# The beginning of a three-part attention and expert kernel: constants moved into the first block, loads reordered and awaited by use

## The chip, the cores and the metric

One core of one Trainium2 chip runs the whole program. The metric is device time in microseconds (us) of one execution. Before the change three runs took 859.69, 860.32 and 865.04 us, so the median is 860.32 us. The engines are named as in the profile: PE is TensorE (matmul), PEld its weight loads, DVE is VectorE, ACT is ScalarE, POOL is GpSimd, SP is SyncE, which here only issues DMAs. SPq, ACTq and so on are the instruction sequencers of these engines.

## What is computed

The input x has 8 batches of 256 rows of 512 features, and there is a context of the same shape. Four residual layers follow each other:

```
x = x + L0_xattn(layernorm(x), ctx)     # latent cross attention, one 128-wide latent
x = x + L0_ffn(layernorm(x))            # gated feed-forward, fp8 operands
x = x + L1_xattn(layernorm(x), ctx, ctx)# 8 heads
x = x + L1_ffn(layernorm(x))            # 8 experts, top 2
```

The change touches only the first layer, and of it only the beginning. For one batch it is

```
theta = theta_w . input2 + theta_b              # input2 = ctx
phi   = phi_w . input1 + phi_b                  # input1 = layernorm(x)
p     = softmax(theta^T . phi)
g     = g_w . input1 + g_b
t     = p . g
h     = relu((t - mean) * rsqrt(var + eps) * ln_gamma + ln_beta)
out   = out_w . h + out_b + ctx
```

## The kernel before, in words

The program is a sequence of blocks. A block holds one instruction stream for each of the five engines, and at a block's end all engines meet at a barrier. The first block (L1794 to L1810) has work for POOL alone: it writes two identity matrices (`ident_b`, `ident_f`), `ones_f`, `mean_f`, `neg_half`, and `empty`, a tile of zeros with row tags, from which SP later clears a table in DRAM (`slots_x`) by the function `fill`. The second block is `latent_attention`, the first layer.

Inside `latent_attention` the eight batches are eight steps of a software pipeline (`steps`), two more drain it. A batch is two tiles of 128 rows. In step i the engines do the projections of batch i, the second half of batch i-1, and the end of batch i-2. Ahead of the first step stands a prologue, and this is where the change lies.

- SP issues the loads in a written order (L135 to L152): the two tiles of x of batch 0 (one DMA), theta's weights, context 0, the weights of phi and g, x of batch 1, context 1 together with the first clearing of `slots_x` (both in `load(1, 1)`, L141 and L1816), gamma, beta, and all the rest of x (3 MB). From then on `load` waits for counts of the running steps.
- ACT loads its function table (L248) and issues five small loads, the biases and `out_w` (`wo`) (L250 to L252).
- DVE waits for x, takes the statistics of batch 0 (`statistics(0)`, L324 to L329), POOL raises the variance to the power -1/2 (`row_rstd(0)`, L432), DVE writes the normalised rows `xln` (L336), ACT rounds them to bf16 (`xh`, L258), DVE takes the remainder (`xl`, L343). Then DVE splits the weights of phi and g in the same way: `wth` (L349, a cast to bf16) and `wtl` (L351, the remainder).
- All eight loads of weights and biases count on one semaphore, `w_in`; PE, ACT, DVE and POOL all wait for all of them (`wait_ge(w_in, 128)`).
- PE starts with theta of batch 0 (L178: fp32, weights `wt[:, 0]`, moving data the context), and goes on with phi (L192: six bf16 matmuls, which read `wth`, `wtl`, `xh`, `xl`), the attention scores (L162) and g (L168).

The semaphores `const_ok` (7 counts) and `zeroed` tell when POOL's constants are there.

Of the kernel before, what the change touches and what calls it, by code (L numbers as in the profile page):

```python
# [8 lines left out]
U32 = mybir.dt.uint32  # L9
ALU = mybir.AluOpType  # L10
# [3 lines left out]
P = 128  # L14
# [23 lines left out]

def latent_attention(nc, X, ident_b, ones_f, mean_f, neg_half, x_in, ctx_in, w, load_ffn, fill, B, S, D, L):

# [8 lines left out]
    DC = S // P  # L49
# [3 lines left out]
    with st:  # L53
# [47 lines left out]
        x_ok = [sem(f"x{k}") for k in range(3)]  # L101
        w_in, norm_in, ones_ok = sem("w_in"), sem("norm_in"), sem("ones_ok")
        ctx_ok = [sem("ctx_ok0"), sem("ctx_ok1")]
# [29 lines left out]
        @block.sync  # L133
        def _(sp):
            sp.dma_start(X[:, 0:DC, :], x_in[:, 0:DC, :]).then_inc(x_ok[0], 16)  # L135
            sp.dma_start(wt[:, 0], w["theta_w"].rearrange("(c p) l -> p c l", p=P)).then_inc(w_in, 16)

            def load(i, par):
                wait(sp, theta_ps, i - 1)
                wait(sp, ctx_added, i - 1)  # L140
                sp.dma_start(ctxb[par][:, :, :], ctx_in[:, bass.ds(i * DC, DC), :]).then_inc(ctx_ok[par], 16)  # L141
                if not isinstance(i, int) or i:
                    fill(sp, (i - 1) * FILL, FILL)

            load(0, 0)
            for k, name in ((1, "phi_w"), (2, "g_w")):
                sp.dma_start(wt[:, k], w[name].rearrange("(c p) l -> p c l", p=P)).then_inc(w_in, 16)
            sp.dma_start(X[:, DC:2 * DC, :], x_in[:, DC:2 * DC, :]).then_inc(x_ok[1], 16)
            load(1, 1)
            sp.dma_start(gamma[:, :], w["ln_gamma"]).then_inc(norm_in, 16)  # L150
            sp.dma_start(beta[:, :], w["ln_beta"]).then_inc(norm_in, 16)
            sp.dma_start(X[:, 2 * DC:B * DC, :], x_in[:, 2 * DC:B * DC, :]).then_inc(x_ok[2], 16)  # L152
            with sp.Fori(1, B // 2) as pair:
                load(pair * 2, 0)
                load(pair * 2 + 1, 1)

        @block.tensor
        def _(pe):
# [81 lines left out]

            pe.wait_ge(w_in, 128)
            pe.wait_ge(ones_ok, 3)
# [3 lines left out]
        def _(act):  # L246

            act.preload_act_table_set("natural_log_exp_and_others")  # L248
            for k, name in enumerate(("theta_b", "phi_b", "g_b")):
                act.dma_start(bias[:, k:k + 1], w[name]).then_inc(w_in, 16)  # L250
            act.dma_start(bias[:, 3:5], w["out_b"]).then_inc(w_in, 16)
            act.dma_start(wo[:, :], w["out_w"]).then_inc(w_in, 16)  # L252

# [6 lines left out]
            high_x(0, 0)  # L260
            act.wait_ge(w_in, 128)
            act.wait_ge(ones_ok, 3)
# [52 lines left out]
        def _(dve):  # L315
            dve.memset(ones_b[:, :], 1.0).then_inc(ones_ok, 1)

            def statistics(i):

                for k in range(3):  # L320
                    if isinstance(i, int) and i == k:
                        dve.wait_ge(x_ok[k], 16)
                for c in range(DC):
                    dve.bn_stats(st6[:, c, :], X[:, bass.ds(i * DC + c, 1), :]).then_inc(stat_ok, 1)  # L324
                for c in range(DC):
# [21 lines left out]
            low_x(0, 0)  # L347
            dve.wait_ge(w_in, 128)
            dve.tensor_copy(wth[:, :, :, :], wt[:, 1:3, :, :]).then_inc(wth_ok, 1)  # L349
            dve.wait_ge(wth_ok, 1)  # L350
            dve.tensor_tensor(wtl[:, :, :, :], wt[:, 1:3, :, :], wth[:, :, :, :], ALU.subtract).then_inc(wtl_ok, 1)  # L351

# [71 lines left out]
        def _(pool):  # L424

            pool.memset(mrow[:, :], 0.0).then_inc(ones_ok, 2)

# [6 lines left out]
            row_rstd(0)  # L434
            pool.wait_ge(w_in, 128)

# [1316 lines left out]
def program(nc, t, out):  # L1753
# [4 lines left out]
    with ExitStack() as st:  # L1758
# [34 lines left out]

        with nc.Block() as block:  # L1794
            @block.gpsimd
            def _(pool):
                pool.memset(ident_b[:, :], 0.0).then_inc(zeroed, 1)
                pool.memset(ident_f[:, :], 0.0).then_inc(zeroed, 1)
                pool.memset(ones_f[:, :], 1.0).then_inc(const_ok, 1)
                pool.memset(mean_f[:, :], 1.0 / P).then_inc(const_ok, 1)  # L1800
                pool.memset(neg_half[:, :], -0.5).then_inc(const_ok, 1)
                pool.wait_ge(zeroed, 2)
                for m in (ident_b, ident_f):
                    pool.affine_select(out=m[:, :], in_=m[:, :], compare_op=ALU.not_equal, fill=1.0, base=0,
                                       pattern=[[-1, P]], channel_multiplier=1).then_inc(const_ok, 1)
                pool.memset(empty[:, :, :], 0.0).then_inc(zeroed, 1)
                pool.wait_ge(zeroed, 3)
                for k in range(2):
                    pool.iota(empty[:, k, R.tag_at:R.tag_at + 1].bitcast(U32), pattern=[[0, 1]], base=(NT + k) * P, channel_multiplier=1)\
                        .then_inc(const_ok, 1)  # L1810
                pool.wait_ge(const_ok, 7)

# [16 lines left out]

        spent = latent_attention(nc, X, ident_b, ones_f, mean_f, neg_half, x_rows, ctx_rows, t, load_ffn, fill, B, S, D, L)  # L1830

# [56 lines left out]
```

## Time and profile before

| | before |
|---|---|
| runs | 859.69, 860.32, 865.04 us |
| profiled execution, its own time | 864.3 us |
| its span | 862.6 us |
| mean granted TensorE clock | 0.942 of full |
| PE busy | 744.9 us (86%) |
| DVE busy | 584.2 us (68%) |
| ACT busy | 399.6 us (46%) |
| POOL busy | 353.8 us (41%) |
| HBM traffic | 120 GB/s over the span |

The profile is of one execution. It ran 4 us above the median of the other three, and 1.7 us of its time lie outside its span. Positions in the trace are us from the span's start. A timeline row reads: start, duration, engine, line of the kernel, operation, output<-input, count, and in brackets the idle time of the engine ahead of it with what ended it. A busy matmul is modelled as pipelined, so overlapping PE rows are usual.

### The profile page before, as it was taken

The page shows a single profiled execution, that of the slowest core. Times are in us where ns is not written, and L with a number is a line of the kernel's source. Part 1 is how long each engine was busy: PE and PEld are TensorE (multiplying, and loading weights), DVE is VectorE, ACT ScalarE, POOL GpSimd, SP SyncE. Part 2 cuts the span into 40 slices and gives each one's busy share as a digit, 9 for nine tenths or more (in the row PEclk, how much of TensorE's full clock was granted, in tenths as well). Part 3 has the DMA queues.
Part 4 walks back from the last instruction along what each step waited for, and adds up shares of the span by engine and source line. Part 5 has one row for each costly group of instructions (what it writes and reads, how often), then busy time and mean ns, then how long its engine had stood idle before and what let it go on. Part 6 is the DMA issues. An engine that isn't in the chain of part 4 may idle for free. (4 is left out here: it accounts for less than half of the span.)

```text
span 862.6 us, 14254 instructions
## 1 busy us (share of the span) xinstructions
PE 744.9 (86%) x4236; PEld 310.4 (36%) x4265; DVE 584.2 (68%) x1098; ACT 399.6 (46%) x744; POOL 353.8 (41%) x354
## 2 busy tenths in 40 slices
PE   3988888829999999979899999999992399999993
PEld 1433344314444444322122222322222255555551
DVE  3668786565858586858788898898848255555552
ACT  1344433306555555436677776776772122222220
POOL 1544556200111113143756658756566023333332
PEclk9899999868999999989999999999995699999998
DMA  7899730022463637813333445434425569888964
GB/s 257 288 106 238 275 125 1 0 89 92 147 215 142 220 135 271 284 38 96 97 98 93 114 96 161 125 91 120 137 107 185 108 109 133 124 124 128 121 100 61
DMA packets 114150, 117.51 MB, mean 136 GB/s; under 512 B 54808, under 2 KB 78232, under 8 KB 113824
## 3 DMA queue, kind: packets, MB, share of 16 engines
q1 hardware_dynamic: 102976, 94.48, 38.5%
q0 software_dynamic: 10384, 22.02, 15.1%
q8 instruction: 36, 0.59, 0.3%
q14 instruction: 34, 0.28, 0.1%
q10 hardware_dynamic: 720, 0.13, 0.1%
HBM read 43.61 MB, written 59.56 MB: 120 GB/s over the span
## 5 line engine op out<-in xcount | busy, mean ns | idle before, releaser
L1235 ACT ACTIVATE t_room<-l_b 128x512 f32<-128x512 f32 x256 | 139.0, 594 | 42.5 <-PE l_b L1130 41.8
L1743 POOL DMA_INDIRECT out<-ex_y,t_tag x39 | 61.2, 1568 | 123.1 <-DMA out<-ex_y,t_tag 61.0
L1639 PE MATMUL ex_hp<-w1h,h_stack 128*128 x312 | 77.4, 317 | 17.2 <-DVE ex_hl L1692 16.7
L1308 DVE TENSOR_REDUCE l_negm<-l_a 128x2 f32<-128x1024 f32 x64 | 75.3, 1220 | 7.9 <-PE l_a L1075 7.9
L1308 DVE TENSOR_REDUCE h_negm<-l_a 128x2 f32<-128x1024 f32 x56 | 66.0, 1221 | 11.9 <-PE l_a L1075 11.9
L1678 ACT ACTIVATE ex_hf<-ex_pre 128x352 f32<-128x352 f32 x39 | 19.4, 496 | 117.5 <-DVE ex_pre L1698 117.5
L1659 PE MATMUL ex_yp<-w2h,ex_ht 128*128 (+1 forms) x215 | 68.9, 380 | 3.2 <-DVE ex_ht L1703 3.0
L598 PE MATMUL f_gp<-f_xt,wg 128*128 128x512 fp8e4 x256 | 67.4, 387 | 3.8 <-ACT f_y L648 2.7
L1141 PE MATMUL l_pv<-t_room,l_vt 128*32 128x512 f32 x512 | 70.3, 622 | 0.0
L1149 PE MATMUL l_sm<-t_room,ones_f 128*32 128x512 f32 x512 | 69.5, 615 | 0.0
L598 PE MATMUL f_up_ps<-f_xt,wg 128*128 128x512 fp8e4 x256 | 67.0, 385 | 0.0
L777 POOL TENSOR_TENSOR X<-X,f_y 128x512 f32<-128x512 f32 x16 | 19.0, 1187 | 94.7 <-ACT f_y L648 94.7
L611 PE MATMUL f_yp<-wl,f_h 128*128 128x512 fp8e4 x256 | 57.3, 379 | 0.0
L709 DVE TENSOR_TENSOR f_prod<-f_gate,f_up 128x512 bf16<-128x512 bf16 x64 | 27.0, 423 | 39.8 <-ACT f_up L637 36.8
L1708 DVE TENSOR_TENSOR ex_hl<-ex_hf,ex_hh 128x352 bf16<-128x352 f32 x39 | 20.5, 526 | 43.9 <-ACT ex_hh L1681 43.9
L1639 PE MATMUL ex_hp<-w1l,h_stack 128*128 x156 | 49.5, 317 | 0.0
L635 ACT ACTIVATE f_gate<-f_gp 128x512 bf16<-128x512 f32 x64 | 38.2, 596 | 20.8 <-PE f_gp L598 20.4
L1659 PE MATMUL ex_yp<-w2l,ex_ht 128*128 (+1 forms) x117 | 44.3, 378 | 3.9 <-DVE ex_ht L1703 2.1
L637 ACT ACTIVATE f_up<-f_up_ps 128x512 bf16<-128x512 f32 x64 | 38.2, 597 | 17.3 <-PE f_up_ps L598 17.2
L1130 PE MATMUL l_b<-h_stack 97*128 97x512 bf16 x128 | 42.2, 406 | 3.9 <-DMA h_stack<-h_mrow 2.9
L1639 PEld LDWEIGHTS ex_hp<-w1h,h_stack 128*128 128x128 bf16 x312 | 30.9, 99 | 32.4 <-issue 17.7
L1716 DVE TENSOR_SCALAR ex_y<-ex_yp,t_tag 128x512 f32<-128x512 f32 x39 | 29.3, 751 | 19.1 <-issue 10.0
(245 smaller groups left out, 1495.2 us busy)
## 6 DMA issues: line engine op xcount, KB each, us to landing
slots_x<-empty SPq DMA_DIRECT2D x8, 2376.0 KB, 11.3
slots_x<-empty SPq DMA_DIRECT2D x7, 2112.0 KB, 13.3
h_stack<-h_parts SPq DMA_DIRECT2D x96, 64.0 KB
l_stack<-l_parts SPq DMA_DIRECT2D x96, 64.0 KB, 2.0
f_stage<-in_w SPq DMA_DIRECT2D x8, 704.0 KB, 4.1
l_ctx<-in_ctx SPq DMA_DIRECT2D x8, 512.0 KB, 7.4
f_stage<-in_w SPq DMA_DIRECT2D x8, 512.0 KB
h_kf<-in_ctx SPq DMA_DIRECT2D x16, 256.0 KB, 3.2
```

Source lines behind the costliest of these rows:

```text
L598: mm = pe.matmul(bank[m % 2][:, :], wg8[:, c, col:col + P], xt8[:, c, :], start=c == 0, stop=c == FC - 1)
L611: mm = pe.matmul(YP[r % 2][:, :], h8[:, m, r * P:(r + 1) * P], wl8[:, m, :], start=m == 0, stop=m == HC - 1)
L635: act.activation(gate[m % 2][:, :], GP[m % 2][:, :], ACT.Gelu_apprx_tanh).then_inc(gate_ok, 1)
L637: act.activation(up[m % 2][:, :], UP[m % 2][:, :], ACT.Copy).then_inc(up_ok, 1)
L1130: pe.matmul(B[t % 2][:, :], stack[u % 2][0:M0 + 1, 0, h, c * P:(c + 1) * P], stack[u % 2][0:M0 + 1, 1, h, :], start=True, stop=True).then_ ...
L1141: mm = pe.matmul(PV[cols, :], VT[u % 2][:, c, cols], weights_at(u, c, h)[:, :], start=c == 0, stop=c == TC - 1)
L1149: mm = pe.matmul(SM[cols, :], ones_f[:, 0:DH], weights_at(u, c, h)[:, :], start=c == 0, stop=c == TC - 1)
L1235: act.activation(weights_at(u, c, h)[:, :], B[t % 2][:, :], ACT.Exp, scale=SCALE).then_inc(b_ok, 1)
L1308: dve.tensor_reduce(negm[u % 2][:, 2 * half:2 * half + 2, j], A[half][:, :, :], AX.X, ALU.max, negate=True)\
L1639: mm = pe.matmul(HP[i % 2][:, 0:H], xt[i % AHEAD][:, xp * FC + f, :], w1p[wp][:, bass.ds(e, 1), f * H:(f + 1) * H], start=k == 0, stop=k = ...
L1659: mm = pe.matmul(YP[i % 2][:, :], ht[i % 2][0:K, n, m, :], w2p[wp][0:K, bass.ds(e, 1), m * D:(m + 1) * D], start=k == 0, stop=k == 3 * HC - 1)
L1743: pool.indirect_dma_start(out=out, out_offset=bass.IndirectOffsetOnAxis(ap=tags[i % TAGS][:, 0:1].bitcast(U32), axis=0), in_=y[i % YS][:, ...
```

## The change

POOL's constants are no longer a block of their own. They become a function, `constants(pool)`, that runs at the head of POOL's stream in the attention block; the block in front of it, and the barrier between them, are gone. What needs the constants waits for `const_ok`: PE ahead of its first matmul, and SP ahead of `load(1, 1)`, whose clearing reads `empty`.

SP's loads: x of batch 0 is two DMAs instead of one, and DVE waits for both. Gamma and beta are issued ahead of context 1 and the first clearing. The single semaphore `w_in` becomes three: `theta_in` (theta's weights, for PE), `w_in` (the weights of phi and g, for POOL), `out_in` (the biases and `wo`, for ACT and DVE). The split of the weights into `wth` and `wtl` moves from DVE to POOL, behind `row_rstd(0)`.

SP's queue at the beginning, before (the first rows of its stream; a name in front of `<-` is the tile that is written):

```order
L133 UNCONDITIONAL_BRANCH [waits barrier_Pool_Activation_PE_DVE_SP_release]
L135 DMA X<-in_x 128x2x512
L136 DMA l_wt<-in_theta_w 128x2x128
L141 DMA l_ctx<-in_ctx 128x2x512
L147 DMA l_wt<-in_phi_w 128x2x128
L147 DMA l_wt<-in_g_w 128x2x128
L148 DMA X<-in_x 128x2x512
L141 DMA l_ctx<-in_ctx 128x2x512
L1816 DMA slots_x<-empty 128x8x528
L150 DMA l_gamma<-in_ln_gamma 128x512
L151 DMA l_beta<-in_ln_beta 128x512
L152 DMA X<-in_x 128x12x512
```

and after the change:

```order
L133 UNCONDITIONAL_BRANCH [waits barrier_Pool_Activation_PE_DVE_SP_release]
L136 DMA X<-in_x 128x512 x2
L137 DMA l_wt<-in_theta_w 128x2x128
L142 DMA l_ctx<-in_ctx 128x2x512
L148 DMA l_wt<-in_phi_w 128x2x128
L148 DMA l_wt<-in_g_w 128x2x128
L149 DMA X<-in_x 128x2x512
L150 DMA l_gamma<-in_ln_gamma 128x512
L151 DMA l_beta<-in_ln_beta 128x512
L142 DMA l_ctx<-in_ctx 128x2x512 [waits const_ok]
L1819 DMA slots_x<-empty 128x8x528
L154 DMA X<-in_x 128x12x512
```

Every load from theta's weights on stands one DMA further back, and the second context, the clearing and the rest of x stand behind gamma and beta. The branch at the top waited in the kernel before for the barrier behind the constants, and now for the one ahead of them, which is not to be seen in these rows.

POOL's stream between the constants and the first step, before:

```order
L1809 IOTA empty 128x1
L1794 UNCONDITIONAL_BRANCH [waits const_ok]
L423 UNCONDITIONAL_BRANCH [waits barrier_Pool_Activation_PE_DVE_SP_gather]
L426 MEMSET l_mrow 128x512
L432 TENSOR_TENSOR l_rstd<-l_veps,neg_half 128x2 [waits l0_veps]
L432 TENSOR_TENSOR l_rstd<-l_veps,neg_half 128x2 [waits l0_ln,l0_veps,l0_w_in]
L458 TENSOR_TENSOR X<-X,l_ctx 128x1024 [waits l0_ln,l0_ctx_ok0]
```

and after the change:

```order
L1812 IOTA empty 128x1
L428 MEMSET l_mrow 128x512 [waits const_ok]
L434 TENSOR_TENSOR l_rstd<-l_veps,neg_half 128x2 [waits l0_veps]
L438 CAST l_wth<-l_wt 128x512 [waits l0_w_in]
L440 TENSOR_TENSOR l_wtl<-l_wt,l_wth 128x512 [waits l0_wth]
L434 TENSOR_TENSOR l_rstd<-l_veps,neg_half 128x2 [waits l0_ln,l0_veps]
L463 TENSOR_TENSOR X<-X,l_ctx 128x1024 [waits l0_ln,l0_ctx_ok0]
```

The block's end and the barrier are gone, and the two operations on the weights have come in from DVE, between the first and the second power of the variance.

The diff, cut to its core:

```diff
--- before.py
+++ after.py
@@ -36,7 +36,7 @@
     eng.nop(nofuse=True)
 
 
-def latent_attention(nc, X, ident_b, ones_f, mean_f, neg_half, x_in, ctx_in, w, load_ffn, fill, B, S, D, L):
+def latent_attention(nc, X, ident_b, ones_f, mean_f, neg_half, x_in, ctx_in, w, load_ffn, fill, constants, const_ok, B, S, D, L):
 
 
 
@@ -99,7 +99,7 @@
         SM = ps("sm", [P, 512])
 
         x_ok = [sem(f"x{k}") for k in range(3)]
-        w_in, norm_in, ones_ok = sem("w_in"), sem("norm_in"), sem("ones_ok")
+        theta_in, w_in, out_in, norm_in, ones_ok = (sem(n) for n in ("theta_in", "w_in", "out_in", "norm_in", "ones_ok"))
         ctx_ok = [sem("ctx_ok0"), sem("ctx_ok1")]
         stat_ok, aggr_ok, rstd_ok, ln_ok, ctx_added = sem("stat"), sem("aggr"), sem("rstd"), sem("ln"), sem("ctxadd")
         wth_ok, wtl_ok, xh_ok, xl_ok = sem("wth"), sem("wtl"), sem("xh"), sem("xl")
@@ -132,8 +132,9 @@
 
         @block.sync
         def _(sp):
-            sp.dma_start(X[:, 0:DC, :], x_in[:, 0:DC, :]).then_inc(x_ok[0], 16)
-            sp.dma_start(wt[:, 0], w["theta_w"].rearrange("(c p) l -> p c l", p=P)).then_inc(w_in, 16)
+            for c in range(DC):
+                sp.dma_start(X[:, c, :], x_in[:, c, :]).then_inc(x_ok[0], 16)
+            sp.dma_start(wt[:, 0], w["theta_w"].rearrange("(c p) l -> p c l", p=P)).then_inc(theta_in, 16)
 
             def load(i, par):
                 wait(sp, theta_ps, i - 1)
@@ -146,9 +147,10 @@
             for k, name in ((1, "phi_w"), (2, "g_w")):
                 sp.dma_start(wt[:, k], w[name].rearrange("(c p) l -> p c l", p=P)).then_inc(w_in, 16)
             sp.dma_start(X[:, DC:2 * DC, :], x_in[:, DC:2 * DC, :]).then_inc(x_ok[1], 16)
-            load(1, 1)
             sp.dma_start(gamma[:, :], w["ln_gamma"]).then_inc(norm_in, 16)
             sp.dma_start(beta[:, :], w["ln_beta"]).then_inc(norm_in, 16)
+            sp.wait_ge(const_ok, 7)
+            load(1, 1)
             sp.dma_start(X[:, 2 * DC:B * DC, :], x_in[:, 2 * DC:B * DC, :]).then_inc(x_ok[2], 16)
             with sp.Fori(1, B // 2) as pair:
                 load(pair * 2, 0)
@@ -238,7 +240,8 @@
                             pe.wait_ge(mrow_ok, i + 1)
                         pe.matmul(ST[c % 2][:, :], ones_b[:, :], mrow[:, :], start=False, stop=True).then_inc(st_ps, 1)
 
-            pe.wait_ge(w_in, 128)
+            pe.wait_ge(const_ok, 7)
+            pe.wait_ge(theta_in, 16)
             pe.wait_ge(ones_ok, 3)
             steps(pe, step)
 
@@ -247,9 +250,9 @@
 
             act.preload_act_table_set("natural_log_exp_and_others")
             for k, name in enumerate(("theta_b", "phi_b", "g_b")):
-                act.dma_start(bias[:, k:k + 1], w[name]).then_inc(w_in, 16)
-            act.dma_start(bias[:, 3:5], w["out_b"]).then_inc(w_in, 16)
-            act.dma_start(wo[:, :], w["out_w"]).then_inc(w_in, 16)
+                act.dma_start(bias[:, k:k + 1], w[name]).then_inc(out_in, 16)
+            act.dma_start(bias[:, 3:5], w["out_b"]).then_inc(out_in, 16)
+            act.dma_start(wo[:, :], w["out_w"]).then_inc(out_in, 16)
 
             def high_x(i, par):
                 act.wait_ge(ln_ok, 2 * i + 2)
@@ -258,7 +261,7 @@
                 act.activation(xh[par][:, :, :], xln[:, :, :], ACT.Copy).then_inc(xh_ok, 1)
 
             high_x(0, 0)
-            act.wait_ge(w_in, 128)
+            act.wait_ge(out_in, 80)
             act.wait_ge(ones_ok, 3)
 
             def step(i, par, half, now, back, back2, more):
@@ -317,10 +320,11 @@
 
             def statistics(i):
 
-                for k in range(3):
-                    if isinstance(i, int) and i == k:
-                        dve.wait_ge(x_ok[k], 16)
                 for c in range(DC):
+                    if isinstance(i, int) and i == 0:
+                        dve.wait_ge(x_ok[0], 16 * DC)
+                    if isinstance(i, int) and i in (1, 2):
+                        dve.wait_ge(x_ok[i], 16)
                     dve.bn_stats(st6[:, c, :], X[:, bass.ds(i * DC + c, 1), :]).then_inc(stat_ok, 1)
                 for c in range(DC):
                     wait_apart(dve, (stat_ok, 2 * i + c + 1))
@@ -345,10 +349,7 @@
             statistics(0)
             normal_rows(0)
             low_x(0, 0)
-            dve.wait_ge(w_in, 128)
-            dve.tensor_copy(wth[:, :, :, :], wt[:, 1:3, :, :]).then_inc(wth_ok, 1)
-            dve.wait_ge(wth_ok, 1)
-            dve.tensor_tensor(wtl[:, :, :, :], wt[:, 1:3, :, :], wth[:, :, :, :], ALU.subtract).then_inc(wtl_ok, 1)
+            dve.wait_ge(out_in, 80)
 
             def low_part(i, n, high, low):
                 dve.wait_ge(high_ok, 2 * i + 1 + n)
@@ -423,6 +424,7 @@
         @block.gpsimd
         def _(pool):
 
+            constants(pool)
             pool.memset(mrow[:, :], 0.0).then_inc(ones_ok, 2)
 
             def row_rstd(i):
@@ -432,7 +434,10 @@
                 pool.tensor_tensor(rstd[:, :], veps[:, :], neg_half[:, 0:DC], ALU.pow).then_inc(rstd_ok, 1)
 
             row_rstd(0)
-            pool.wait_ge(w_in, 128)
+            pool.wait_ge(w_in, 32)
+            pool.tensor_copy(wth[:, :, :, :], wt[:, 1:3, :, :]).then_inc(wth_ok, 1)
+            pool.wait_ge(wth_ok, 1)
+            pool.tensor_tensor(wtl[:, :, :, :], wt[:, 1:3, :, :], wth[:, :, :, :], ALU.subtract).then_inc(wtl_ok, 1)
 
             def step(i, par, half, now, back, back2, more):
                 if back:
@@ -1791,24 +1796,22 @@
         zeroed = st.enter_context(nc.semaphore("zeroed"))
         const_ok = st.enter_context(nc.semaphore("const_ok"))
 
-        with nc.Block() as block:
-            @block.gpsimd
-            def _(pool):
-                pool.memset(ident_b[:, :], 0.0).then_inc(zeroed, 1)
...
-                pool.wait_ge(const_ok, 7)
+        def constants(pool):
+            pool.memset(ident_b[:, :], 0.0).then_inc(zeroed, 1)
+            pool.memset(ident_f[:, :], 0.0).then_inc(zeroed, 1)
+            pool.memset(ones_f[:, :], 1.0).then_inc(const_ok, 1)
+            pool.memset(mean_f[:, :], 1.0 / P).then_inc(const_ok, 1)
+            pool.memset(neg_half[:, :], -0.5).then_inc(const_ok, 1)
+            pool.wait_ge(zeroed, 2)
+            for m in (ident_b, ident_f):
+                pool.affine_select(out=m[:, :], in_=m[:, :], compare_op=ALU.not_equal, fill=1.0, base=0,
+                                   pattern=[[-1, P]], channel_multiplier=1).then_inc(const_ok, 1)
+            pool.memset(empty[:, :, :], 0.0).then_inc(zeroed, 1)
+            pool.wait_ge(zeroed, 3)
+            for k in range(2):
+                pool.iota(empty[:, k, R.tag_at:R.tag_at + 1].bitcast(U32), pattern=[[0, 1]], base=(NT + k) * P, channel_multiplier=1)\
+                    .then_inc(const_ok, 1)
+            pool.wait_ge(const_ok, 7)
 
         def fill(sp, first, tiles):
 
@@ -1827,7 +1830,7 @@
             pool.dma_start(wg8[:, :, :], t["w_gating"]).then_inc(w8_ok, 16)
             pool.dma_start(wl8[:, :, :], t["w_linear"].rearrange("(m p) d -> p m d", p=P)).then_inc(w8_ok, 16)
 
-        spent = latent_attention(nc, X, ident_b, ones_f, mean_f, neg_half, x_rows, ctx_rows, t, load_ffn, fill, B, S, D, L)
+        spent = latent_attention(nc, X, ident_b, ones_f, mean_f, neg_half, x_rows, ctx_rows, t, load_ffn, fill, constants, const_ok, B, S, D, L)
 
         EW = ExpertWeights(sb, D, H, E)
         first = ExitStack()
```

## Rows read from the trace of the kernel before

**Rows 1.** The waits of SP's queue, 0 to 5 us: who waited for whom, total, times, longest.

```profile
SPq L1794 <- PEq L1794: 2.9, 1, 2.9
```

**Rows 2.** Timeline of POOL: the first and the last of the constants.

```profile
0.81 0.20 POOL L1797 MEMSET ident_b<- 128x128 bf16 x1 [0.29 <-POOLq L1883]
...
3.07 0.20 POOL L1809 IOTA empty<- 128x1 uint32 x2
```

**Rows 3.** Timeline of the first issues on SP's queue.

```profile
3.75 0.46 SPq L135 DMA_DIRECT2D X<-in_x  x1
...
4.78 0.47 SPq L141 DMA_DIRECT2D l_ctx<-in_ctx  x1
...
5.80 0.47 SPq L147 DMA_DIRECT2D l_wt<-in_g_w  x1
...
12.64 0.66 SPq L152 DMA_DIRECT2D X<-in_x  x1
```

**Rows 4.** DMA issues one by one: engine, count, KB, us from issue to landing.

```profile
X<-in_x SPq DMA_DIRECT2D x1, 512.0 KB, 4.8
...
l_ctx<-in_ctx SPq DMA_DIRECT2D x1, 512.0 KB, 6.5
...
l_wt<-in_g_w SPq DMA_DIRECT2D x1, 128.0 KB, 6.2
...
X<-in_x SPq DMA_DIRECT2D x1, 3072.0 KB, 17.7
```

**Rows 5.** Timeline of the first batch, from x's landing to the scores.

```profile
8.58 1.29 DVE L324 BATCH_NORM_STATS2 l_st<-X 128x6 f32<-128x512 f32 x2 [4.57 <-DMA X<-in_x]
...
11.21 1.00 DVE L336 TENSOR_SCALAR l_xln<-X,l_mv,l_rstd 128x512 f32<-128x512 f32 x2 [0.85 <-POOL l_rstd L432]
...
12.24 1.06 ACT L258 ACTIVATE l_xh<-l_xln 128x1024 bf16<-128x1024 f32 x1 [7.21 <-DVE l_xln L336]
...
12.61 3.78 PE L178 MATMUL l_r<-l_ctx,l_wt 128*128 128x512 f32 x4 [12.61 <-DMA l_wo<-in_out_w]
...
13.33 1.23 DVE L343 TENSOR_TENSOR l_xl<-l_xln,l_xh 128x1024 bf16<-128x1024 f32 x1 [1.12 <-ACT l_xh L258]
...
14.93 0.69 DVE L351 TENSOR_TENSOR l_wtl<-l_wt,l_wth 128x512 bf16<-128x512 f32 x1
...
16.18 0.63 PE L192 MATMUL l_r<-l_xh,l_wth 128*128 128x512 bf16 x1
...
20.22 0.59 PE L162 MATMUL l_a<-l_phi_h,l_theta_h 128*128 128x512 bf16 x2 [1.65 <-DVE l_phi_l L355]
```

**Rows 6.** Groups of instructions by form, POOL, whole span.

```profile
L848 POOL TENSOR_TENSOR h_parts<-h_kf,h_parts 128x512 bf16<-128x512 f32 x8 | 9.5, 1183 | 5.6 <-ACT h_parts L840 5.1
...
L1483 POOL CAST l_parts<-h_qf 128x512 bf16<-128x512 f32 x7 | 4.3, 610 | 10.0 <-DVE h_qf L831 10.0
```

**Rows 7.** The tile `l_dev`, 45 to 130 us: duration ns min/median/max.

```profile
L367 DVE TENSOR_TENSOR l_dev<-l_dev x5: 1082/1169/1241, 49.5 to 125.6; 128x1 f32<-128x1 f32 x5
L369 DVE TENSOR_TENSOR l_dev<-l_dev,l_tmv x5: 159/160/161, 50.8 to 126.8; 128x1 f32<-128x1 f32 x5
```

**Rows 8.** Timeline of `l_dev` and POOL beside it.

```profile
49.50 1.24 DVE L367 TENSOR_TENSOR l_dev<-l_dev 128x1 f32<-128x1 f32 x1
...
49.47 1.26 POOL L445 TENSOR_TENSOR l_psa<-l_psa,l_psb 128x512 f32<-128x512 f32 x1
```

**Rows 9.** Timeline of the second step and the third: pv, and what uses the late loads.

```profile
30.68 1.88 PE L178 MATMUL l_r<-l_ctx,l_wt 128*128 128x512 f32 x4
...
33.70 3.60 PE L203 MATMUL l_pv<-l_pt,l_gx 128*128 128x512 f32 x8
...
35.28 1.28 DVE L324 BATCH_NORM_STATS2 l_st<-X 128x6 f32<-128x512 f32 x2
...
51.23 5.38 PE L203 MATMUL l_pv<-l_pt,l_gx 128*128 128x512 f32 x8
```

**Rows 10.** Busy time in a stretch: PE, PEld, DVE, ACT, POOL, then PEclk, DMA share, GB/s.

```profile
51.99:55.41 3.42, 3.42 (x5) 1.34 (x4) 1.79 (x6) 0.00 (x0) 2.21 (x3) 0.53 0.74 87
```

More of the change, by code:

```diff
@@ L1792, in program @@
         const_ok = st.enter_context(nc.semaphore("const_ok"))
-        with nc.Block() as block:
-            @block.gpsimd
-            def _(pool):
-                pool.memset(ident_b[:, :], 0.0).then_inc(zeroed, 1)
[L1798 to L1810, printed above, removed]
-                pool.wait_ge(const_ok, 7)
+        def constants(pool):
[14 more added lines that the diff above has]
+            pool.wait_ge(const_ok, 7)
         def fill(sp, first, tiles):
```

## The prediction, made before the changed kernel was run

> **What bounds the kernel now.** I read first the page's busy shares and its mean granted clock: PE is busy 86% of the span, so the steady state belongs to PE and to the chains around it. But the change moves nothing in any steady state; it rearranges the prologue. So the question is only when the first phi matmul can start, because behind it stand PE's own queue and eight steps that follow each other at a fixed distance. I then went through the waits of SP, the timeline up to the first phi, and the landing times of the loads.
>
> Nothing is loaded in the first 3.75 us. SP stands 2.9 us at the barrier [rows 1], whose other side is POOL: its constants run from 0.81 to 3.27 [rows 2], and 0.48 later the engines are in the next block. Then SP issues, about 0.51 us apart [rows 3]. From there three branches meet at phi [rows 4, 5]:
> - x lands 4.8 after its issue; statistics start at 8.58, `xln` at 11.21, ACT's `xh` at 12.24, DVE's `xl` at 13.33 to 14.56.
> - PE's theta starts at 12.61, released by the load of `wo`, since PE waits for all weights and biases together. Context 0, which theta needs, was there at 4.78 + 6.5 = 11.28. Theta holds PE for 3.57 (12.61 to the first phi matmul at 16.18), at the lower of the two clock levels: its four matmuls read 3.78, and 1.88 in the second step [rows 9].
> - DVE splits the weights behind `xl`, and is done at 14.93 + 0.69 = 15.62, half a microsecond ahead of theta's end.
>
> So PE with theta is the last of the three, by 0.56 us, and theta was held 1.33 us by a load that it doesn't use.
>
> **The change, part by part.** All positions are estimates from those rows.
>
> *Barrier gone.* SP stops waiting at 3.75 - 2.9 = 0.85. That agrees with POOL, which gets through the same first barrier at 0.81 today. Every load's issue moves by 2.9. The constants still take until 3.27, now beside the loads. Who waits for them: PE, at theta (not before 8), and SP at the second context. SP reaches that wait after nine issues, at 0.85 + 9 x 0.51 = 5.4 or later, so it costs nothing.
>
> *x in two halves.* The second half is issued at 0.85 + 0.51 = 1.36, and DVE needs both. If bytes are the limit the pair lands when the whole did, at 0.85 + 4.8 = 5.65; if the time from issue is, at 1.36 + 4.8 = 6.16. I take the middle, 5.9; no row says which. Then by the distances of today: `xln` at 5.9 + 2.63 = 8.53, `xh` at 9.56, `xl` could start at 10.65, and would end at 11.88.
>
> *Theta released by its own loads.* Context 0 is the fourth or now the fifth in time (two halves of x, theta's weights, then it): issue at 0.85 + 3 x 0.51 = 2.38, landing at 8.9; 8.4 if bytes decide (11.28 - 2.9). Theta ends, for PE's next matmul, at 8.9 + 3.57 = 12.45, or 11.95.
>
> *Split of the weights on POOL.* g's weights are issued at 0.85 + 5 x 0.51 = 3.40 and land at 9.6 (6.2 later), or at 5.80 + 6.2 - 2.9 = 9.1. POOL is free then, the power having been done by 8.5. Casts of just this form take it 0.61, two-input operations with bf16 output 1.18 [rows 6]. So `wth` is done at 10.2 and `wtl` runs from 10.27 to 11.45. By itself that is hidden behind theta.
>
> *But DVE's `xl` falls into it.* Look at the squaring of two numbers per partition at L367: with nothing in its way it would cost what L369 costs, 0.16. It takes 1.17 at the median of 5 [rows 7], and in the one shown it starts at 49.50 and ends at 50.74, just behind POOL's addition, 49.47 to 50.73 [rows 8]. DVE's operation with two SBUF inputs stood until POOL's was through. `xl` is such an operation, ready at 10.65, while `wtl` runs to 11.45. So I let it start at 11.45 and end at 12.68, and phi starts 0.1 behind, at about 12.8, now 0.35 behind theta's end. The Trainium skill's page "GPSIMD Engine Reference", section "1. Specifications", says that GpSimd's SBUF interfaces are shared with VectorE, with contention for DVE instructions that have two SBUF inputs; the squaring, 1.17 against 0.16, agrees. The rule speaks against moving the split off DVE. Without it phi would start at theta's end, 12.45, and the sum below would be 3.7 in place of 3.4.
>
> *The sum.* Phi's first matmul moves from 16.18 to 12.8: a gain of 3.4 us. Bounds: all loads limited by bytes and `xl` unhindered give theta's end at 11.95, a gain of 4.2. The late x with `xl` first (10.9 to 12.1), and POOL's `wtl` made to wait for it, give 12.1 + 1.2 = 13.3, and a gain of 2.8. I keep 3.4, because the wait at L367 happened in 5 of 5.
>
> *DVE without the split* (14.56 to 15.62) gains nothing of its own: DVE's next work waits for ACT's theta.
>
> *The later loads.* The rest of x was issued at 12.64 and landed 17.7 later, at 30.3 [rows 3, 4]; its first use is the statistics at 35.28 [rows 9], which didn't wait. That use moves to 31.9. The bytes ahead of that load are the same, and begin 2.9 earlier, so it should land near 27.4, and even a landing as late as today is in time. Context 1 has 512 KB more ahead of it now (gamma and beta), but is still ahead of the clearing and of that same load; theta of the second step, 30.68 today [rows 9], moves to 27.3. I cost both at nothing; the cover is over 1.5 us even at the worst.
>
> *All the rest* is the same work at a fixed distance behind phi, so it shifts. The loads of the running steps are issued on counts of steps, and shift too.
>
> Against the profiled execution's own time: 864.3 - 3.4 = 860.9. That execution ran 4.0 above the median of the runs; the prediction is for the median: 860.3 - 3.4 = 856.9 us, or 0.4% less. What this kernel's measurement can tell from no change is taken as 1%, 8.6 us, so this gain is "within 1%".
>
> **The clock as noise.** The granted clock falls in pieces of some 3.4 us: in 51.99:55.41 it was 0.53 with PE busy all the time [rows 10], and the same eight matmuls of pv, 3.60 us in one step, took 5.38 there [rows 9]. So one such piece laid on a busy PE costs 1.8 us. Moving the beginning by 3.4 us lays them anew; the three runs, 859.7 to 865.0, lie as far apart as three pieces would put them.
>
> **Rivals.**
> - *One such piece fewer, or one more.* 856.9 - 1.8 = 855.1, or 858.7. The range of the runs speaks for both, and nothing for one above the other: 0.12 and 0.13.
> - *The clock stays low through the second step.* This one ends slower. Theta now starts 3.7 earlier, and PE idles 0.35 between it and phi, where it ran on without a gap today. If that gap, with the one ahead of the scores (1.65 today [rows 5], unchanged), keeps the clock at its lower level up to pv of the second step, that is three more pieces on a busy PE, 5.4 - 3.4 = 2.0 us lost: 862.3 us. It decides from the second additional piece on. Against: 0.35 us is small beside the gap that PE already has there, and six phi matmuls follow it at once. 0.06.
> - *The loads don't start sooner.* If SP and ACT need until 3.75 for something other than the barrier (the start of the queues, say), only theta's earlier release is left: it starts at 11.28 + 0.51 = 11.8 and ends at 15.4, but `xl`, behind `wtl`, ends at 12.68 + 2.9 = 15.6, and phi starts at 15.7. Gain 0.5, at 859.8; with the split made last, none, 860.3. For: no row shows a load before 3.75. Against: the profile puts SP's whole wait down to the barrier, with 0.51 from issue to issue at once behind it [rows 1, 3]. 0.08.
> - *A late load stalls the second or third step*, by 1 to 2 us of the 3.4: 858 to 859. 0.03.
>
> The forecast itself, with gains of 2.8 to 4.2, has 0.58.
>
> **How the numbers follow.** The time is the forecast's, 856.9. For the range I take the forecast (856.1 to 857.5), the piece fewer and more (855.1, 858.7) and the late start (859.8 to 860.3), with 0.7 either way for the median of a few runs: 854.3 to 860.8. It leaves out the slower rival and two pieces fewer. Faster by over 1% would need 851.7, five microseconds beyond the forecast: 0.02. Slower by over 1% needs 869, which no case gives: 0.02. The rest, 0.96, is within 1%.
>
> **What would show each step.** SP's first issue at 0.85 and not 3.75. First `bn_stats` at 5.7 to 6.2. Theta at 8.4 to 8.9 with the context's load as its releaser. `wtl` on POOL from about 10.3, 1.2 long. DVE's `xl` lengthened from 1.23 to about 2.0, or started late, with its end just 1.2 behind POOL's; phi's first matmul at 12.8. If `xl` reads 1.23 beside a running `wtl`, the sharing was wrong here. SP should not wait for `const_ok`. The statistics of batch 2 near 31.9 with no wait for a DMA, and later stages all 3.4 earlier but for pieces of the clock. It is wrong if SP doesn't start sooner, or if the distance gained at phi is gone by the second step's theta.

## The result, and the profile after

| | before | changed |
|---|---|---|
| runs | 22, median 860.77 us (857.92 to 867.04) | 22, median 859.64 us (853.91 to 864.11) |
| ratio | | 0.9965, 95% interval 0.9948 to 0.9982 |
| profiled execution, span | 864.3, 862.6 us | 864.11, 862.4 us |
| mean granted clock | 0.942 | 0.939 |

The ratio is 3.0 us off 860.8, with an interval from 1.5 to 4.5; 3.4 was forecast. The medians in the table are only 1.1 us apart and the plain means of the same runs 2.4 (861.5 and 859.2), so the size of the gain is known to a few us at best. Where ratios are given here and below, executions in which the whole program ran slow (such as one of 1010 us and one of 2551) are left out. The profiled execution of the changed kernel is its slowest run, so the two profiled spans hide the gain. It has to be read stage by stage.

The changed kernel's timeline up to phi and the scores (start, duration, engine, line, operation):

```profile
0.81 0.87 SPq L136 DMA_DIRECT2D X<-in_x  x2
...
3.22 0.47 SPq L148 DMA_DIRECT2D l_wt<-in_g_w  x1
...
5.44 1.29 DVE L328 BATCH_NORM_STATS2 l_st<-X 128x6 f32<-128x512 f32 x2 [4.36 <-DMA X<-in_x]
...
7.33 3.38 SPq L154 DMA_DIRECT2D X<-in_x  x1
8.07 1.00 DVE L340 TENSOR_SCALAR l_xln<-X,l_mv,l_rstd 128x512 f32<-128x512 f32 x2 [0.85 <-POOL l_rstd L434]
9.08 3.75 PE L180 MATMUL l_r<-l_ctx,l_wt 128*128 128x512 f32 x4 [9.08 <-DMA l_ctx<-in_ctx]
9.10 1.06 ACT L261 ACTIVATE l_xh<-l_xln 128x1024 bf16<-128x1024 f32 x1 [7.01 <-DVE l_xln L340]
10.19 1.22 DVE L347 TENSOR_TENSOR l_xl<-l_xln,l_xh 128x1024 bf16<-128x1024 f32 x1 [1.12 <-ACT l_xh L261]
10.26 1.63 POOL L438 CAST l_wth<-l_wt 128x512 bf16<-128x512 f32 x1 [2.22 <-DMA l_wt<-in_g_w]
11.96 1.15 POOL L440 TENSOR_TENSOR l_wtl<-l_wt,l_wth 128x512 bf16<-128x512 f32 x1
...
13.17 0.43 PE L194 MATMUL l_r<-l_xh,l_wth 128*128 128x512 bf16 x1 [0.34 <-POOL l_wtl L440]
...
16.34 0.59 PE L164 MATMUL l_a<-l_phi_h,l_theta_h 128*128 128x512 bf16 x2 [1.65 <-DVE l_phi_l L356]
```

Against [rows 3, 5]: SP's first issue is at 0.81 in place of 3.75, x's statistics start at 5.44 in place of 8.58, theta at 9.08 in place of 12.61, released now by the context. Phi starts at 13.17 in place of 16.18. Two rows carry the surprise. POOL's cast, which reads 0.61 elsewhere [rows 6], takes 1.63; it began 0.07 behind DVE's `xl` and ended 0.48 behind its end. And phi's releaser is POOL's `wtl`, not `xl`, though PE would have been free at 9.08 + 3.57 = 12.65.

The context's landing, x's rest, and SP's waits in the changed kernel:

```profile
l_ctx<-in_ctx SPq DMA_DIRECT2D x1, 512.0 KB, 6.8
...
l_wo<-in_out_w ACTq DMA_DIRECT2D x1, 128.0 KB, 7.3
l_wt<-in_g_w SPq DMA_DIRECT2D x1, 128.0 KB, 7.0
...
X<-in_x SPq DMA_DIRECT2D x1, 3072.0 KB, 20.5
```

```profile
SPq L1886 <- PEq L1886: 0.5, 1, 0.5
```

SP has no wait for `const_ok` in the first 12 us; the row in the second block is all that it waits there. g's weights took 7.0 us to land, not 6.2 [rows 4], so POOL's split began 0.66 late. The rest of x was issued at 7.33 and landed at 27.8; its use didn't wait:

```profile
25.70 1.88 PE L180 MATMUL l_r<-l_ctx,l_wt 128*128 128x512 f32 x4
...
28.71 3.60 PE L205 MATMUL l_pv<-l_pt,l_gx 128*128 128x512 f32 x8
...
30.30 1.27 DVE L328 BATCH_NORM_STATS2 l_st<-X 128x6 f32<-128x512 f32 x2
```

These answer to [rows 9]: theta of the second step starts at 25.70 in place of 30.68. Phi gained 3.01, but this gained 4.98. What lies between is the clock, in two places. From phi to the scores it took 3.17 us in place of 4.04 (16.34 less 13.17; 20.22 less 16.18 in [rows 5]): of the six phi matmuls, five read 0.38 here, and four read 0.63 before. From the scores to this theta it took 9.36 in place of 10.46, and the clock shows it. The stretches (PE, PEld, DVE, ACT, POOL busy, then PEclk, DMA share, GB/s), the changed kernel first, then a third profile of the kernel before:

```profile
21.00:28.00 7.00, 6.36 (x27) 2.58 (x28) 2.34 (x4) 4.09 (x7) 1.43 (x2) 1.00 1.05 389
```

```profile
21.00:28.00 7.00, 5.74 (x35) 3.31 (x33) 4.73 (x12) 1.20 (x3) 3.01 (x2) 0.55 1.04 387
```

Before, the granted clock was at its lower level nearly throughout (0.55), and a bf16 score matmul read 0.61 to 0.64; after, it was at the upper one (1.00), and the same matmul read 0.39.

The other end of the program takes some back. The last scatters of POOL, the kernel before, then the changed one:

```profile
846.40 1.57 POOL L1743 DMA_INDIRECT out<-ex_y,t_tag  x1 [2.72 <-DMA out<-ex_y,t_tag]
851.99 1.56 POOL L1743 DMA_INDIRECT out<-ex_y,t_tag  x1 [4.02 <-DMA out<-ex_y,t_tag]
853.85 1.56 POOL L1743 DMA_INDIRECT out<-ex_y,t_tag  x1 [0.30 <-issue]
```

```profile
846.20 1.57 POOL L1748 DMA_INDIRECT out<-ex_y,t_tag  x1 [2.90 <-DMA out<-ex_y,t_tag]
851.69 1.56 POOL L1748 DMA_INDIRECT out<-ex_y,t_tag  x1 [3.91 <-DMA out<-ex_y,t_tag]
853.55 1.56 POOL L1748 DMA_INDIRECT out<-ex_y,t_tag  x1 [0.30 <-issue]
```

DVE's last result was begun 3.8 us earlier (847.6 and 851.4), and the last scatter 0.3 earlier: in this one execution the chain of scatters, each waiting for one before it to land, ran that much longer. Two further profiles of either kernel tell what of this is the kernel and what the execution.

### The profile page after: what moved, and what is told of

The parts are those of the page before. It is cut to its first block and busy times, and to the rows that moved or that the text cites. A ratio compares the mean times of both kernels' runs of the same rounds, so it can differ in the third digit from the quotient of the medians.

```text
span 862.4 us, 14275 instructions
## 1 busy us (share of the span) xinstructions
PE 747.3 (87%) x4265; PEld 308.8 (36%) x4265; DVE 582.7 (68%) x1096; ACT 399.5 (46%) x744; POOL 358.5 (42%) x356
## 5 line engine op out<-in xcount | busy, mean ns | idle before, releaser
L1644 PE MATMUL ex_hp<-w1h,h_stack 128*128 x312 | 78.4, 321 | 17.2 <-DVE ex_hl L1697 16.7
L1664 PE MATMUL ex_yp<-w2h,ex_ht 128*128 (+1 forms) x234 | 76.2, 380 | 4.7 <-DVE ex_ht L1708 4.4
L1713 DVE TENSOR_TENSOR ex_hl<-ex_hf,ex_hh 128x352 bf16<-128x352 f32 x39 | 20.5, 525 | 43.9 <-ACT ex_hh L1686 43.9
L1721 DVE TENSOR_SCALAR ex_y<-ex_yp,t_tag 128x512 f32<-128x512 f32 x39 | 29.3, 750 | 20.0 <-issue 12.5
## 6 DMA issues: line engine op xcount, KB each, us to landing
slots_x<-empty SPq DMA_DIRECT2D x7, 2112.0 KB, 13.3
```

The source lines that it names most:

```text
L1644: mm = pe.matmul(HP[i % 2][:, 0:H], xt[i % AHEAD][:, xp * FC + f, :], w1p[wp][:, bass.ds(e, 1), f * H:(f + 1) * H], start=k == 0, stop=k = ...
L1664: mm = pe.matmul(YP[i % 2][:, :], ht[i % 2][0:K, n, m, :], w2p[wp][0:K, bass.ds(e, 1), m * D:(m + 1) * D], start=k == 0, stop=k == 3 * HC - 1)
```

## The experiments

All were profiled; "ratio" is against the kernel before in the same series on the same chip, with its 95% interval. Three series follow (experiments 1 to 4, 5 to 8, 9 to 12), and the kernel before had medians of 868.2, 872.4 and 867.8 us in them, so times of different series aren't compared with each other.

**1. The barrier alone.** On the kernel before:

```diff
-        with nc.Block() as block: ...            # the constants' block
+            constants(pool)                      # at the head of POOL's stream
+            pe.wait_ge(const_ok, 7)
+            sp.wait_ge(const_ok, 7)              # ahead of load(1, 1)
```

> The kernel before with one part of the change: the constants move to the head of POOL's stream in the attention block, the block and barrier in front are gone, and PE and SP (ahead of the second context) wait for const_ok. Loads in their old order, one semaphore for all weights, split on DVE. Theory (the barrier is nearly all of it): SP issues at 0.81, every landing is 2.94 us earlier, theta starts at 12.61 - 2.94 = 9.67, released by wo as before, phi's first matmul at 16.18 - 2.94 = 13.24, as near to the start as in the full change (13.17); gain 2.9 us. Rival (the releases by use and the new order carry a part of their own): phi in the full change would be at least half a microsecond ahead of this kernel's.

Phi at 13.28, theta at 9.73 behind `wo`; ratio 0.9967 (0.993 to 1.0004). The theory held to 0.04 us, and the first profile of the full change is only 0.11 ahead. But that profile was a late one, as experiments 6 and 10 showed. The interval of the time reaches no change.

```profile
9.73 3.75 PE L179 MATMUL l_r<-l_ctx,l_wt 128*128 128x512 f32 x4 [9.73 <-DMA l_wo<-in_out_w]
10.32 1.22 DVE L345 TENSOR_TENSOR l_xl<-l_xln,l_xh 128x1024 bf16<-128x1024 f32 x1 [1.12 <-ACT l_xh L260]
...
13.28 0.52 PE L193 MATMUL l_r<-l_xh,l_wth 128*128 128x512 bf16 x1
```

**2. All but the barrier.** The changed kernel with the constants' block back in front (`with nc.Block()` and no call in POOL's stream).

> The changed kernel with the constants' block and its barrier put back, all else as changed. Theory: SP issues at 3.75, everything up to phi is 2.94 us later than in the changed kernel, phi's first matmul at 13.17 + 2.94 = 16.1 against 16.18 before; no gain that can be told from none. Rival (the rest of the change has a worth of its own): phi at 15.6 or earlier and 0.5 us or more gained.

Phi at 15.34, 0.8 ahead of the kernel before; the rival's number. Theta was released by the context at 11.42. Ratio 0.9989 (0.9949 to 1.0029), which tells nothing. The rows show DVE and POOL in the other order, the cast first:

```profile
12.58 0.61 POOL L437 CAST l_wth<-l_wt 128x512 bf16<-128x512 f32 x1 [2.06 <-DMA l_wt<-in_g_w]
12.68 1.58 DVE L347 TENSOR_TENSOR l_xl<-l_xln,l_xh 128x1024 bf16<-128x1024 f32 x1 [1.12 <-ACT l_xh L261]
13.27 2.01 POOL L439 TENSOR_TENSOR l_wtl<-l_wt,l_wth 128x512 bf16<-128x512 f32 x1
```

The cast has its 0.61. `xl`, begun beside it, takes 1.58 in place of 1.23, and `wtl`, begun beside `xl`, takes 2.01 in place of 1.15. Whoever comes second stands until about the end of the first: from there `xl` still took 1.07 and `wtl` 1.02, a little under their own 1.23 and 1.15.

**3. The split back on DVE.** On the changed kernel:

```diff
             low_x(0, 0)
+            dve.wait_ge(w_in, 32)                # and cast, subtract as before
-            pool.wait_ge(w_in, 32)               # and POOL's cast, subtract
```

> The changed kernel with the split of the weights put back on DVE, behind xl, waiting for w_in only. Theory (POOL and DVE cannot read at once, so that xl held POOL's cast up): xl ends at 11.41 as in the changed kernel, the cast takes 0.42 and the remainder 0.69, done at 12.55; theta, started at 9.08 by the context, ends for PE's next matmul at 12.65, and phi starts at about 12.65, 0.5 us ahead of the changed kernel. Rival (something else makes the end of the split, such as the landing of g's weights at 10.26 alone): phi at 13.1 or later here too.

Phi at 12.11; the loads landed early here (x 5.01, context 8.29), so the number isn't the forecast's, but its make-up is: DVE's split ended at 12.05, theta's next matmul was due at 11.86, phi stood 0.06 behind the split. Ratio 0.9896 (0.9831 to 0.996), from only three executions.

**4. Weights ahead of the context.** On the changed kernel, the loads of `phi_w` and `g_w` stand ahead of `load(0, 0)`.

> The changed kernel with the loads of phi's and g's weights issued ahead of context 0. Theory (sharing): g's weights land near 8.2, so POOL's cast and subtraction run before xl starts at 10.19; the cast reads near 0.61 and not 1.63, the subtraction 1.15 to 1.2, unless DVE's xln (8.07 to 9.07) holds them up; the context lands 0.6 us later, at about 9.7, theta ends for phi at 13.25, and phi starts there. Rival (the cast is slow at this place for another reason, such as DMA writing into SBUF or being POOL's first of its kind): it reads 1.63 again although no DVE operation with two inputs runs beside it.

```profile
7.63 0.60 POOL L438 CAST l_wth<-l_wt 128x512 bf16<-128x512 f32 x1
7.69 2.11 DVE L340 TENSOR_SCALAR l_xln<-X,l_mv,l_rstd 128x512 f32<-128x512 f32 x2 [0.85 <-POOL l_rstd L434]
8.31 1.21 POOL L440 TENSOR_TENSOR l_wtl<-l_wt,l_wth 128x512 bf16<-128x512 f32 x1
9.31 3.75 PE L180 MATMUL l_r<-l_ctx,l_wt 128*128 128x512 f32 x4 [9.31 <-DMA l_ctx<-in_ctx]
```

The cast reads 0.60 here, so the rival (slow at this place by itself) is out. But now DVE's `xln` pays, 2.11 in place of 1.00: an operation with one tensor input from SBUF is held up too. It isn't the order of loads: experiment 12 has the same one and nothing on POOL at that time, and there the two `xln`, from 7.65, take 1.00. Phi at 12.86, just 3.55 behind theta. Ratio 0.9997 (0.9961 to 1.0034).

**5 and 6. The same kernels again.** The kernel before, then the changed one.

> The kernel before, profiled a second time, to see what varies by itself. Theory (the half-speed piece in the first batch is a matter of where the clock's changes fall in this run): theta at 12.6, phi at 16.2, and then either 14.5 us from phi to the second step's theta (with the clock low on the way) or about 12.7 (without). Rival (it belongs to the late start): 14.5 again.

> The changed kernel, profiled a second time. Theory: x and context 0 land within 0.5 us of the first profile's 5.4 and 9.1, POOL's cast and DVE's xl again exclude each other, so phi starts at 12.5 to 13.3. The distance from phi to the second step's theta is 12.5 where the clock stays up and 14.5 where it falls, and the last scatter ends 12 to 16 us behind PE's last matmul of the experts.

The kernel before: phi at 15.87, and 14.46 to the second step's theta, with the clock low again. The changed one: phi at 11.91, then 13.02. Theta started at 7.83, since the context landed in 5.5 us and not 6.8, and `wtl` took 2.17 behind `xl`:

```profile
8.99 0.61 POOL L438 CAST l_wth<-l_wt 128x512 bf16<-128x512 f32 x1 [1.53 <-DMA l_wt<-in_g_w]
9.62 1.23 DVE L347 TENSOR_TENSOR l_xl<-l_xln,l_xh 128x1024 bf16<-128x1024 f32 x1 [1.12 <-ACT l_xh L261]
9.68 2.17 POOL L440 TENSOR_TENSOR l_wtl<-l_wt,l_wth 128x512 bf16<-128x512 f32 x1
11.91 0.61 PE L194 MATMUL l_r<-l_xh,l_wth 128*128 128x512 bf16 x1 [0.32 <-POOL l_wtl L440]
```

I had expected 12.5 to 13.3, so the spread of the landings was larger than taken: theta of the changed kernel started at 7.8, 8.7 and 9.1 in three profiles. The last scatter was over at 853.1, 14.1 us behind the start of the experts' last hidden matmul (839.0), as expected.

**7. PE warmed up.** On the changed kernel:

```diff
+            pe.wait_ge(warm_ok, 1)               # a tile of ones, written by DVE
+            for k in range(24):
+                pe.matmul(ST[k % 2][:, :], warm[:, 0:P], warm[:, :], start=True, stop=True)
             pe.wait_ge(const_ok, 7)
```

> The changed kernel with 24 matmuls of 128x512 on a tile of ones, written to a bank that is overwritten later, ahead of PE's first waits (their results are not used). Theory: they bring the clock up before theta, which takes 1.9 in place of 3.75 us; but phi still waits for the split on POOL, so it starts at 12.8 to 13.2 as in the changed kernel, and gains nothing by itself; what it may gain is the clock behind phi. Rival (theta is the bound at phi): phi near 11.5.

Theta took 1.88 from 8.77 on, straight behind the 24 matmuls, and phi started at 12.49, held by POOL's `wtl` (10.34, 2.09 long beside `xl`). So theta's length wasn't the bound any more; the pair was. Ratio 0.9939 (0.9902 to 0.9976).

**8. Three edits together.** Weights first, the split on DVE between `xln` and `xl`, and the warm-up.

> Three edits on the changed kernel together: the weights of phi and g are loaded ahead of context 0, the split is on DVE between xln and xl (in the time in which ACT rounds xh), and the 24 matmuls ahead of theta. Theory: the split is done by 10.2, xl ends near 11.4, theta runs 9.3 to 11.2 at the upper clock level; phi starts at 11.4, 1.8 us ahead of the changed kernel and 4.8 ahead of the kernel before. Rival (the warm-up does not raise the clock in time, or holds theta up): phi at 12.9.

```profile
1.53 7.98 PE L246 MATMUL l_st<-l_warm 128*128 128x512 bf16 x24 [1.53 <-DVE l_warm L323]
...
8.49 0.42 DVE L357 CAST l_wth<-l_wt 128x512 bf16<-128x512 f32 x1
8.61 1.06 ACT L265 ACTIVATE l_xh<-l_xln 128x1024 bf16<-128x1024 f32 x1 [6.52 <-DVE l_xln L345]
8.95 0.69 DVE L359 TENSOR_TENSOR l_wtl<-l_wt,l_wth 128x512 bf16<-128x512 f32 x1
9.70 1.23 DVE L352 TENSOR_TENSOR l_xl<-l_xln,l_xh 128x1024 bf16<-128x1024 f32 x1
9.86 1.96 PE L181 MATMUL l_r<-l_ctx,l_wt 128*128 128x512 f32 x4 [0.35 <-DMA l_ctx<-in_ctx]
11.66 0.38 PE L195 MATMUL l_r<-l_xh,l_wth 128*128 128x512 bf16 x1
```

Phi at 11.66, near the 11.4 forecast and the earliest of all fourteen profiles. The split lies between `xln` and the end of ACT's rounding of `xh`, and nothing on DVE is stretched. In this profile, of an execution of 877.84 us, the clock was low again from 17.2 to 20.5 us. Ratio 0.9953 (0.992 to 0.9987).

**9 to 12. The kernel before once more, the changed one and the split on DVE with more executions, and the new order without the warm-up.**

> The kernel before, profiled a third time. The three profiles with the barrier so far (two of this kernel, one of the changed one with the barrier put back) had the clock low for some 6.8 us in the first batch, and the six without it and without a warm-up of PE did not. Theory (it goes with the late start): 14.5 us from phi to the second step's theta again. Rival (chance): about 12.7 to 13.2, with the clock up.

> The changed kernel, profiled and timed beside the two below. Theory: phi at 11.9 to 13.2, after the POOL/DVE pair, and 12.5 to 13.2 us from phi to the second step's theta, with the clock up. Rival (chance): 14.5, with the clock low.

> The changed kernel with the split put back on DVE behind xl, timed with more runs than before. Theory: phi at theta's end or 0.1 behind DVE's last operation of the split, 0.2 to 0.6 us ahead of the changed kernel in the same state of the loads; a time within 1 us of the changed kernel's. Rival (the one large gain measured before was real): 5 us or more faster than the changed kernel on the same chip.

> The changed kernel with the weights of phi and g loaded ahead of context 0 and the split on DVE between xln and xl, without the matmuls that warm PE up. Theory: all of DVE's work is done at 10.9 to 11.4, but theta, started by the context at 9.3 to 9.9 at the lower clock level, holds PE for 3.57, and phi starts at 12.9 to 13.4: the new order is worth nothing without the warm-up. Rival (PE's clock is not the bound there): phi at 11.7 as in the kernel with all three edits.

The kernel before: phi 16.34, then 14.52 with the clock low. The changed one: phi 12.74, then 13.19 with the clock up, ratio 0.9976 (0.9943 to 1.001); its cast took 1.61 beside `xl`:

```profile
9.76 1.23 DVE L347 TENSOR_TENSOR l_xl<-l_xln,l_xh 128x1024 bf16<-128x1024 f32 x1 [1.12 <-ACT l_xh L261]
9.84 1.61 POOL L438 CAST l_wth<-l_wt 128x512 bf16<-128x512 f32 x1 [2.24 <-DMA l_wt<-in_g_w]
```

The split on DVE: phi 12.48, 0.06 behind DVE's last operation; ratio 0.9946 (0.9913 to 0.998), an interval that overlaps the changed kernel's in the same series, so the larger gain of experiment 3 isn't confirmed. The new order without the warm-up: DVE done at 11.0, theta from 9.55, phi at 13.09, as the theory had it; ratio 0.9958 (0.9929 to 0.9986).

Put together, the kernels with the barrier and those without, in us from the span's start (first of theta and phi in the first step; theta of the second step; first matmul of the feed-forward layer; first head-attention score maximum of DVE; first matmul of the experts; span):

| profile | theta | phi | 2nd theta | FFN | heads | experts | span |
|---|---|---|---|---|---|---|---|
| before, 1 | 12.61 | 16.18 | 30.68 | 196.5 | 382.2 | 680.2 | 862.6 |
| before, 2 | 12.29 | 15.87 | 30.33 | 196.2 | 381.9 | 687.0 | 871.2 |
| before, 3 | 12.77 | 16.34 | 30.86 | 196.7 | 382.4 | 683.1 | 866.1 |
| barrier back | 11.42 | 15.34 | 29.95 | 195.9 | 381.4 | 685.3 | 867.6 |
| changed, 1 | 9.08 | 13.17 | 25.70 | 191.7 | 377.4 | 676.3 | 862.4 |
| changed, 2 | 7.83 | 11.91 | 24.93 | 188.0 | 373.7 | 678.1 | 860.5 |
| changed, 3 | 8.68 | 12.74 | 25.93 | 186.6 | 371.9 | 678.7 | 861.6 |
| barrier alone | 9.73 | 13.28 | 25.94 | 192.1 | 377.6 | 681.7 | 864.1 |
| split on DVE, 1 | 8.29 | 12.11 | 25.32 | 186.0 | 371.2 | 675.6 | 857.7 |
| split on DVE, 2 | 8.70 | 12.48 | 24.97 | 190.8 | 376.3 | 678.7 | 861.4 |
| weights first | 9.31 | 12.86 | 26.04 | 189.0 | 373.1 | 677.2 | 860.6 |
| new order, cold | 9.55 | 13.09 | 25.76 | 191.8 | 377.4 | 683.6 | 867.4 |

## Why the prediction was right, and where its steps were not

**Barrier gone: right.** SP at 0.81, forecast 0.85. It is most of the change: alone it moved phi by 2.90 of some 3.5.

**x in two halves: earlier than both bounds.** The statistics began at 5.44, 4.86 and 5.01 in the changed kernel's profiles; forecast 5.9, bounds 5.65 and 6.16. Whole x with the barrier gone landed at 5.57, and the three profiles of before, less 2.94, give 5.64, 5.18 and 5.15. So the 4.8 us taken for the landing came from a late profile, and splitting costs nothing and perhaps saves 0.3; the term was a cost of 0.25. That the whole order of loads differs too keeps this from being shown.

**Theta released by its own loads: right as to the release, not as to the place.** Forecast 8.4 to 8.9, measured 9.08, 7.83, 8.68. Not reckoned was how far a landing strays between executions.

**The split on POOL, and `xl` beside it: the exclusion right, its order not.** I let `wtl` start at 10.27 and go first, and `xl`, ready at 10.65, wait, for phi at 12.8. In all three profiles `xl` started first, by 0.06 to 0.08 us, since x had landed early; it kept its 1.23 and POOL stood: the cast 1.63, the subtraction 2.17, the cast 1.61. That is the case that I had priced at the lower bound (gain 2.8). This is the step that failed: the wait was laid on DVE, as in [rows 7, 8] (where DVE works on one number per partition, not two as I wrote), and it fell on POOL. Experiments 2 and 4 have it the other way, 1.58 for `xl` and 2.11 for `xln` when POOL was first. From the start of `xl` to phi I had 2.15 us; it took 2.98, 2.29 and 2.98, so 0.6 more at the mean, while `xl` started 0.8 earlier (at 9.86, the mean of three, and not 10.65). Phi came out at 13.17, 11.91 and 12.74, mean 12.61, against 16.13 for the kernel before: 3.5 us, for 3.4 forecast. That the sum came out so near is in part luck, two errors that cancelled.

**DVE's release gains nothing: right,** as was the cost of nothing for `const_ok`, x's rest and context 1.

**"All the rest shifts": wrong, to the good at first.** Up to the second step's theta the mean gain is 5.1 (30.62 against 25.52), 1.6 more than at phi. The clock makes it: the four profiles with the barrier had it low in 21 to 28 us and took 14.5 to 14.6 from phi to that theta; the eight without barrier and warm-up had it up and took 12.5 to 13.2. The low piece of 21 to 28 us is worth 1.1 of the 1.6: from the scores to that theta it is 10.46 to 10.48 us in the four and 9.36 to 9.41 in the eight. The other 0.5 is phi's own matmuls, of which fewer ran at the lower level (4.0 us from phi to the scores before, 3.17, 3.66 and 3.83 in the changed kernel's profiles). I had called the pieces of the clock noise about which nothing can be said. In the first batch they are not: four of four against none of eight. At the feed-forward layer the three profiles each differ by 7.7 (196.5 against 188.8). Why the clock falls with the late start and not with the early one stays open: the idle times of PE behind phi are the same, 1.65 and 1.26 us, in both. Nor is a late start needed for it: experiment 8, with the earliest phi of all and PE at work from 1.53 us on, had such a piece in 17.2 to 20.5. The low pieces later in the first layer are not so regular (in 51 to 56 us of all four with the barrier; in 46 to 52 of four of the eight, and nowhere between 15 and 60 us in the other four).

**Given back later.** Of 7.7 us at the feed-forward layer, 7.8 are left where head attention begins, 5.7 at the experts and 5.1 at the end, as means of three. The head attention took 298.0, 305.1 and 300.7 us before and 298.9, 304.4 and 306.8 after: it varies more by itself than the mean difference of 2.1. In the first profile the tail of the scatters took 3.5 more; in the two others it did not (last scatter 2.4 and 2.3 us behind DVE's last result, against 2.4, 4.3 and 2.5 before, and 5.9 there). Nothing ties either to the change.

**The size.** The timed ratios, 0.9965 (0.9948 to 0.9982) and 0.9976 (0.9943 to 1.001), are 3.0 and 2.1 us; the three profiles a side say 5.1. With single executions 5 to 10 us apart these agree, and the timed ones weigh more. That the gain is real rests on the first interval; that it is more than phi's 3.5 isn't shown, nor that it is as much. The forecast was a median of 856.9, and 859.64 was measured: inside the range, but nearer to what two rivals gave (858.7 and 859.8) than to the forecast. The ends of the range, 854.3 and 860.8, are also 0.1 and 0.2 off what the cases named give with 0.7 either way (854.4 and 861.0). So the time by itself doesn't tell the forecast from these rivals; the rows do.

**Of the rivals,** the late start is out, by SP's first issue at 0.81; a piece fewer is what happened in the first batch, but it was one of 6.8 us, as long as two, and worth 1.1 us, where I had put 1.8 on each; the clock staying low happened in the kernel before, not in the changed one, where PE idled 0.32 to 0.34 ahead of phi, as reckoned.

**A better version?** The three edits of experiment 8 bring phi 1 us further forward than the changed kernel's mean, and the split on DVE 0.3. Their ratios, 0.9953 and 0.9946, are the lowest of the well-sampled ones, but all intervals overlap that of the changed kernel. None can be called better by time.

## What to carry to other kernels

Where engines wait at a barrier for one engine's constants, moving the constants behind it and awaiting them by a count was worth the whole wait at the first phi (2.9 us in one profile), since the loads set the prologue; the releases by use and the new order of loads, with the split moved, gave some 0.7 more there. In the time of the whole program neither part can be told from nothing by itself (0.9967, to 1.0004, and 0.9989, to 1.0029); only all together can. Before you move work from DVE to POOL to free DVE, look at what DVE runs at that moment on SBUF: the two took turns here, and the work cost most of its time again. And read the clock's rows behind a moved start: the shift can come out larger or smaller than what was moved.

## What the runs showed that was not expected

POOL and DVE hold each other up also where the one that waits has a single tensor input. A cast on POOL (one input) took 1.61 and 1.63 beside `xl` in place of 0.61; two `xln` on DVE (one tensor input each) took 2.11 in place of 1.00 beside POOL's cast and subtraction. The Trainium skill's page "Advanced Engine Details and Errata", section "VectorE Performance Modes", says that GpSimd instructions and VectorE's two-port modes block each other, which fits `xln`; whether it ran in such a mode no row here shows.

The time from a load's issue to its landing strays: the same 512 KB of context 0, fourth in SP's queue, took 6.8 us in one execution and 5.5 in another.

24 dense matmuls ahead of the first real one halved theta, 1.88 and 1.96 us in place of 3.75. In experiment 8 theta still stood 0.35 for the context behind them, so they didn't delay it; in experiment 7 it came straight behind them, and a small delay isn't excluded. Without them (experiment 12) theta alone was the bound of the best order.
